# Turning x, y and exp(q) in 32x32 blocks on VectorE, and three iterations for each batch, in a two-layer linear attention

## The chip, the cores and the metric

The kernel runs on one core of one Trainium2 chip. The metric is the device time of one execution in microseconds (us). It is written with one instruction stream for each engine and semaphores between them: TensorE (PE), VectorE (DVE), ScalarE (ACT), GpSimd (POOL) and SyncE (SP), whose only work here is to issue DMAs.

## The reference

Two layers of the same kind run on x, 8 batches of 512 rows and 512 columns (f32), with a condition of 8 x 1024 that gives a scale and a shift for each batch. Layer 0 has 16 heads of 32 columns, layer 1 has 8 of 64. Cut to one layer:

```python
xn = layernorm(x) * norm_scale + norm_bias
q, k, v = xn @ Wq + bq, xn @ Wk + bk, xn @ Wv + bv
k = where(mask, -inf, k)                  # layer 1: k + (1 - mask) * -1e6
v = where(mask, 0, v)                     # layer 1: v * mask
q = softmax(q per head, axis=columns of the head)
k = softmax(k per head, axis=sequence)
attn = einsum('bhse,bhsd->bhed', k, v)
y = einsum('bhtd,bhed->bhte', q, attn)
scale, shift = split(silu(emb) @ film_emb_W + film_emb_b, 2)
h = layernorm(y) * (1 + scale) + shift
return x + silu(h) @ film_out_W + film_out_b
```

## The kernel before

**Tiles.** A batch of x is four tiles of 128 rows (t) by 512 columns; turned, it is four chunks of 128 columns (c) by 512 rows. TensorE contracts over the partition axis, so each operand of a projection must be turned: xT for K, V and Q, the turned q (qT) for the attention, and the turned y for the output projection O. Each f32 operand of a projection is split into a high part (rounded to TensorE's fast 32-bit format) and a low part (the rest), and a product is three passes, high by high, low by high, high by low (L434): 12 products of 512 columns make one tile, 48 a projection.

**Order.** A Python loop, `run_iterations` (L267), writes the order of each engine by hand; the batches 1 to 6 of each layer are a hardware loop (`Fori`) on every engine. There are 16 iterations i, 8 a layer. Iteration i has K, V and Q of batch i, its key-value sums (L643: k_exp by v, 64 or 128 small products into psum_k), the attention built from them by VectorE (L1027 to L1048), the transposes of q on TensorE (`turn_q`, L667), four attends (`attend`, L679: qT by the attention, with a column that sums exp(q)), and between them the four O tiles of batch i-1. The transposes of y (`turn_y`, L507) stand in K and V of the next iteration.

**Turning.** q and y are turned by TensorE with the identity matrix, 128 x 128 each, 16 a batch, into the PSUM tile psum_t; ScalarE copies q from there (L1248) and makes the silu gate from y there (L1187). x is turned by TensorE (L494) in layer 1 and for batches 0 and 1 of layer 0 (ten batches of sixteen in all); for the others the host gives x already turned as well, and VectorE normalises it with rows of mean and 1/std that went through a small tensor in HBM (L752, L754).

**The other engines in an iteration.** VectorE normalises y (L911); takes the greatest k of each tile (L963); makes the key's shift from it, a chain of small steps (L883 to L904, here called the chain) between two block transposes (L875, L904); splits the gate's low parts (L917); subtracts the shift from k (L985); takes the statistics of the next x; biases each q tile out of psum_w (L996) and takes its maxima (L999); builds the attention; adds the output tiles to the residual (L924); and scales each tile of y with the reciprocal of its sum (L1072, L1074). ScalarE masks v out of psum_w (L1218), takes exp of k and q (L1242), scales xT, and makes high parts. GpSimd subtracts q's maxima (L1357), adds the output's bias to the residual (L1323), makes the low parts of x (L1289) and 1/std. psum_w has two halves, used in turn by V, Q and O: a product waits until the tile before last has been taken from its half.

## Time and profile before

| what | value |
|---|---|
| time, median of 3 runs | 865.17 us (863.83 to 866.48) |
| the profiled execution | 866.68 us |
| its span, 16137 instructions | 864.6 us |
| DMA queues | 24700 packets, 78.31 MB |
| granted clock of TensorE, mean | 0.996 |

The span is the profiled time from the first instruction to the last; 2.1 us lie around it. The durations below come from this one execution. Busy time on TensorE is counted by modelled ends of pipelined matmuls: two rows that overlap are read by the distance of their starts. The granted clock is a share of 2.4 GHz: 1.00 is 2.4 GHz and 0.50 is 1.2 GHz.

### The profile page before, as it was taken

What the parts mean: (1) busy time and instruction counts of PE and PEld (TensorE: products, weight loads), DVE (VectorE), ACT (ScalarE), POOL (GpSimd) and SP (SyncE); (2) the same over time, 40 slices, a digit from 0 to 9 for tenths busy, and PEclk for the clock granted to TensorE, in tenths of its full rate; (3) what the DMA queues carried; (4) which work ended last, traced back from release to release, by engine and by line L of the source; (5) the groups of instructions that cost most, each with busy time, mean ns of one, the idle gap of its engine ahead of it and who ended that gap; (6) DMA issues with size and microseconds to landing.
All of it is one profiled execution on the core that took longest, in us unless ns stands there. A gap on an engine that the chain in (4) does not pass through costs nothing.

```text
span 864.6 us, 16137 instructions
## 1 busy us (share of the span) xinstructions
PE 851.0 (98%) x5915; PEld 744.5 (86%) x5915; DVE 619.2 (72%) x1324; ACT 397.6 (46%) x607; POOL 283.6 (33%) x323
## 2 busy tenths in 40 slices
PE   7999999999999999999999999999999999999998
PEld 6678888888888888888888888898888988888887
DVE  6768787877778787777886775667657675575864
ACT  5145445534544553454753634544344433444433
POOL 2032432405243240524313343231433304343520
PEclk8999999999999999999999999999999999999999
DMA  8772222132312213240220403003030120301202
GB/s 270 278 263 99 75 114 81 51 119 73 146 73 111 84 49 121 73 194 14 101 101 1 158 2 133 13 6 139 0 146 0 49 97 0 146 0 58 88 2 97
DMA packets 24700, 78.31 MB, mean 91 GB/s; under 512 B 5464, under 2 KB 5464, under 8 KB 18784
## 3 DMA queue, kind: packets, MB, share of 16 engines
q1 hardware_dynamic: 24672, 77.93, 24.1%
q8 instruction: 18, 0.29, 0.1%
q14 instruction: 10, 0.08, 0.0%
HBM read 61.12 MB, written 16.80 MB: 90 GB/s over the span
## 4 chain that ended last, share of the span: by engine, by line
PE 96%; DVE 2%; DMA 1%; issue 0%; ACT 0%; POOL 0%; SPq 0%; DVEq 0%
PE psum_w L434 58%; PE psum_k L434 20%; PE psum_k L679 6%; PE psum_t L507 3%; PE psum_t L667 3%; PE psum_k L643 3%; PE psum_t L494 2%; DVE y L1074 1%; DMA x_in<-in_x 1%; PE psum_t L459 0%; PE psum_k L459 0%; DVE q_rsum L1072 0%; DVE y_stats L1081 0%; DVE w_low_q L761 0%; PE psum_w L667 0%
## 5 line engine op out<-in xcount | busy, mean ns | idle before, releaser
L1289 POOL TENSOR_TENSOR xT_low<-xT,xT_high 128x512 fp32r<-128x512 f32 x60 | 78.2, 1303 | 168.2 <-ACT xT_high L1148 166.8
L1187 ACT ACTIVATE gate<-psum_t,film_shift,film_scale 128x512 f32<-128x512 f32 x60 | 46.5, 775 | 132.2 <-PE psum_t L507 104.8
L434 PE MATMUL psum_k<-w_high_k,xT_high 128*128 128x512 f32 x256 | 102.0, 399 | 4.5 <-DVE y L1074 2.4
L996 DVE TENSOR_TENSOR q<-psum_w,bias_q 128x512 f32<-128x512 f32 x64 | 44.3, 692 | 80.4 <-PE psum_w L434 80.4
L1273 POOL TENSOR_SCALAR x_var<-x_moments 128x4 f32<-128x4 f32 x15 | 3.4, 228 | 293.1 <-DVE x_moments L733 293.1
L434 PE MATMUL psum_w<-w_high_v,xT_high 128*128 128x512 f32 x256 | 98.7, 386 | 0.0
L434 PE MATMUL psum_k<-w_low_k,xT_high 128*128 128x512 f32 x256 | 98.4, 384 | 0.0
L434 PE MATMUL psum_k<-w_high_k,xT_low 128*128 128x512 f32 x256 | 98.2, 383 | 0.0
L434 PE MATMUL psum_w<-w_high_q,xT_high 128*128 128x512 f32 x256 | 97.5, 381 | 0.0
L434 PE MATMUL psum_w<-w_low_v,xT_high 128*128 128x512 f32 x256 | 97.1, 379 | 0.0
L434 PE MATMUL psum_w<-w_high_v,xT_low 128*128 128x512 f32 x256 | 97.1, 379 | 0.0
L434 PE MATMUL psum_w<-w_low_q,xT_high 128*128 128x512 f32 x256 | 97.1, 379 | 0.0
L434 PE MATMUL psum_w<-w_high_q,xT_low 128*128 128x512 f32 x256 | 97.1, 379 | 0.0
L434 PE MATMUL psum_w<-w_high_o,gT_high 128*128 128x512 f32 x240 | 95.0, 396 | 0.0
L434 PE MATMUL psum_w<-w_low_o,gT_high 128*128 128x512 f32 x240 | 91.0, 379 | 0.0
L434 PE MATMUL psum_w<-w_high_o,gT_low 128*128 128x512 f32 x240 | 91.0, 379 | 0.0
L1242 ACT ACTIVATE q<-q 128x512 f32<-128x512 f32 x64 | 40.4, 631 | 107.2 <-POOL q L1357 107.2
L1218 ACT ACTIVATE v<-psum_w,v_mask 128x512 f32<-128x512 f32 x64 | 44.3, 692 | 91.6 <-PE psum_w L434 91.6
L1357 POOL TENSOR_TENSOR q<-q,q_max 128x512 f32<-128x512 f32 x64 | 67.6, 1075 | 40.4 <-DVE q_max L999 40.4
L1323 POOL TENSOR_TENSOR x_res<-x_res,bias_o 128x512 f32<-128x512 f32 x60 | 75.7, 1293 | 5.7 <-DMA x_res<-x_between_layers 5.7
L1248 ACT COPY qT<-psum_t 128x512 f32<-128x512 f32 x60 | 32.3, 590 | 83.1 <-PE psum_t L667 83.1
L963 DVE SCALAR_TENSOR_TENSOR k_max<-psum_k,k_mask,k_max 128x512 f32<-128x512 f32 x48 | 36.0, 751 | 46.6 <-PE psum_k L434 43.0
(159 smaller groups left out, 1850.1 us busy)
## 6 DMA issues: line engine op xcount, KB each, us to landing
x_in<-x_between_layers SPq DMA_DIRECT2D x9, 1024.0 KB, 4.8
x_res<-in_x SPq DMA_DIRECT2D x8, 1024.0 KB, 6.8
x_between_layers<-x_res SPq DMA_DIRECT2D x8, 1024.0 KB, 3.8
x_in<-in_x SPq DMA_DIRECT2D x7, 1024.0 KB, 4.8
x_res<-x_between_layers SPq DMA_DIRECT2D x7, 1024.0 KB, 6.7
out_x<-x_res SPq DMA_DIRECT2D x7, 1024.0 KB, 3.8
x_in<-in_x_turned SPq DMA_DIRECT2D x6, 1024.0 KB, 5.1
raw_weights<-in_L_cond_film_emb_W SPq DMA_DIRECT2D x4, 1024.0 KB, 7.1
```

What stands on the lines that cost most here:

```text
L434: mm = pe.matmul(bank, lhs[:, c, rows_of_tile], alternating(rhs[w][:, c, :]), start=(c == 0 and n == 0), stop=(c == CHUNKS - 1 and n == 2))
L507: mm = pe.transpose(psum_t[:, c % 2, t, :], y[:, t, c * P:(c + 1) * P], ident[:, :])
L679: mm = pe.matmul(y_psum_of(t)[:, g, 0:BCOLS], qT[:, t, g, :], att_of[layer][:, g, :], start=True, stop=True)
L963: dve.scalar_tensor_tensor(out=k_max[:, :], in0=psum_k[:, t, :], scalar=mask, in1=k_max[:, :], op0=ALU.add, op1=ALU.max).then_inc(k_max_do ...
L996: dve.tensor_tensor(q[:, t, :], psum_w[:, t % 2, :], bias_q[:, :], ALU.add)\
L1187: act.activation(gate[:, c % 2, :], psum_t[:, c % 2, :, :].rearrange("p t s -> p (t s)"), ACT.Silu, scale=film_scale[:, cond, c:c + 1].rea ...
L1218: act.activation(v_of(layer)[:, t, :, 0:width], psum_w[:, t % 2, :].rearrange("p (h n) -> p h n", n=width), ACT.Copy, scale=v_mask[:, bass ...
L1242: act.activation(q[:, t, :], q[:, t, :], ACT.Exp).then_inc(q_exp_ready, 1)
L1248: act.copy(qT[:, t, :, :].rearrange("p c s -> p (c s)"), q_bank(i, t)).then_inc(qT_ready, 1)
L1289: pool.tensor_tensor(xT_low[:, c, :], xT[:, c % 2, :], xT_high[:, c, :], ALU.subtract)\
L1323: pool.tensor_tensor(x_biased, x_biased, bias_o[:, :], ALU.add)\
L1357: pool.tensor_tensor(rows_q, rows_q, q_max[:, t, 0:HEADS[layer]].unsqueeze(2) .to_broadcast([P, HEADS[layer], width]), ALU.subtract).then_ ...
```

## The change

**Three iterations for a batch.** Iteration i now has the projections of batch i in the order K, Q, V; the four attends of batch i-1, after the tiles K2, K3, Q0 and Q1 (a letter and a digit are a projection and its tile t); the key-value sums of batch i; and the output projection of batch i-2. The attention of batch i is built while O of batch i-2 runs. Iterations 0, 1, 2, 6, 7 and 8, 9, 10, 14, 15 are written out, and 3 to 5 and 11 to 13 are loops. The last batch's attends stand between its neighbours' O tiles at the end.

**Turning.** x, y and exp(q) are turned in 32 x 32 blocks within the partitions by VectorE (L784, L793, L801: four instructions of 128 x 512 each a batch), into free parts of raw and k_exp. Sixteen DMAs (`deal`) then put the blocks of one tensor to their partitions, so that xT, yT or qT stands as it did. A deal is issued by SyncE, 16 transfers of 32 partitions x 4 chunks x 128 values (64 KB) each; there are three in an iteration. Before the block transposes ScalarE normalises x and y in their rows (L1294, L1300), with a scale and an offset that GpSimd makes. The last batch's q and y are still turned by TensorE, as are x of batches 0 and 1. The turned x of the host and the rows through HBM are gone.

**What goes with it.** GpSimd takes over the gate's low parts and those of layer 1's weights from VectorE. The gate is made in place in yT. The attends write psum_t, which holds one tile of theirs, where before they had two places in psum_k. Layer 1's weights go through one slot.

```diff
+            def deal(to, blocks, dealt):
+                of_quadrant = blocks.rearrange("p (c d) t j -> p c d (t j)", c=CHUNKS)
+                for frm in range(P // QUAD):
+                    for d in range(P // QUAD):
+                        sp.dma_start(to[d * QUAD:(d + 1) * QUAD, :, frm * P:(frm + 1) * P],
+                                     of_quadrant[frm * QUAD:(frm + 1) * QUAD, :, d, :]).then_inc(dealt[frm], 16)
...
+            def projections(layer, i, att_layer):
...
+                for t in range(TILES):
+                    if t == 0:
+                        pe.wait_ge(att_ready, i)
...
+                        project(i, t, K, psum_k[:, t, :])
+                    if t >= 2:
+                        attend(i - 1, t - 2, att_layer)
...
+                for t in range(TILES):
...
+                    project(i, t, Q, psum_w[:, t % 2, :])
+                    if t < 2:
+                        attend(i - 1, t + 2, att_layer)
...
+                for t in range(TILES):
+                    if t < 2:
+                        pe.wait_ge(q_biased, TILES * i + t + 3)
+                    else:
+                        pe.wait_ge(v_ready, TILES * i + t - 1)
+                    project(i, t, V, psum_w[:, t % 2, :])
...
+            def turn_y_blocks(j, t):
+                if t == 0:
+                    dve.wait_ge(y_normed, TILES * (j + 1))
...
+                dve.transpose(xy_blocks[:, :, t, :], y[:, t, :].rearrange("p (b j) -> p b j", j=QUAD))\
+                   .then_inc(y_blocked, 1)
+            def turn_q_blocks(i, t):
+                if t == 0:
+                    dve.wait_ge(q_exp_ready, TILES * (i + 1))
+                    dve.wait_ge(att_done, i + 1)
+                dve.transpose(q_blocks[:, :, t, :], q[:, t, :].rearrange("p (b j) -> p b j", j=QUAD))\
+                   .then_inc(q_blocked, 1)
-            def normalise_y(j):
-                dve.wait_ge(y_scale_done, 2 * (j + 1))
-                dve.wait_ge(y_moments_done, TILES * (j + 1))
-                for t in range(TILES):
-                    dve.tensor_scalar(y[:, t, :], y[:, t, :], y_moments[:, t, 0:1], y_rstd[:, t:t + 1],
-                                      ALU.subtract, ALU.mult).then_inc(yn_ready, 1)
...
+                take_y(j, att_layer, 3)
+                take_q(i, layer, 1)
+                stats_of_y(j, 3)
+                for t in range(TILES):
+                    moments_of_y(j, t)
+                take_q(i, layer, 2)
+                k_shift_of(i, layer)
+                take_q(i, layer, 3)
+                for t in range(TILES):
+                    turn_y_blocks(j, t)
+                shift_k(i)
+                if normalises_x(i):
+                    x_stats_of(i + 2)
+                if not fixed(i, LAST):
+                    for t in range(TILES):
+                        turn_q_blocks(i, t)
+                if gives_out(i) and not fixed(i, LAST):
+                    add_residual(i - 2, 0)
+                sum_attention(i, layer)
...
+            def low_of_gate(j):
+                high, low = gated_of(j)
+                for c in range(CHUNKS):
+                    pool.wait_ge(g_high_ready, CHUNKS * j + c + 1)
+                    pool.tensor_tensor(low[:, c, :], yT[:, c, :], high[:, c, :], ALU.subtract).then_inc(g_low_ready, 1)
```

**How the instructions move.** On TensorE, in the loop over the batches of layer 0, the second and the third O tile stood so before, with eight transposes of q between them:

```order
L434 MATMUL psum_w<-w_high_o,gT_high 128x512
L434 MATMUL psum_w<-w_low_o,gT_high 128x512
L434 MATMUL psum_w<-w_high_o,gT_low 128x512
L667 MATMUL psum_t<-ident,q 128x128 x8
L434 MATMUL psum_w<-w_high_o,gT_high 128x512
L434 MATMUL psum_w<-w_low_o,gT_high 128x512
```

Now nothing stands between the O tiles, and between K2 and K3 (and three more pairs) there is an attend of the batch before (here in iteration 1, whose x stands in the gate's tiles):

```order
L489 MATMUL psum_k<-w_low_k,gT_high 128x512
L489 MATMUL psum_k<-w_high_k,gT_low 128x512
L581 MATMUL psum_t<-att,qT 128x132 x4
L489 MATMUL psum_k<-w_high_k,gT_high 128x512
L489 MATMUL psum_k<-w_low_k,gT_high 128x512
```

So the attends went from behind the sums of their own batch to the K and Q tiles of the next, and the transposes of q are gone.

Before, the products ahead of the key-value sums were those of the last Q tile, so that v had been masked a whole projection earlier:

```order
L434 MATMUL psum_w<-w_high_q,xT_high 128x512
L434 MATMUL psum_w<-w_low_q,xT_high 128x512
L434 MATMUL psum_w<-w_high_q,xT_low 128x512
L637 REGISTER_ALU
L643 MATMUL psum_k<-v,k_exp 32x34 x64
```

Now they are those of V3:

```order
L489 MATMUL psum_w<-w_high_v,xT_high 128x512
L489 MATMUL psum_w<-w_low_v,xT_high 128x512
L489 MATMUL psum_w<-w_high_v,xT_low 128x512
L720 MATMUL psum_k<-v,k_exp 32x34 x64
L489 MATMUL psum_w<-w_high_o,gT_high 128x512
```

V has moved behind Q: the mask of v tile 3 on ScalarE now stands between the last product and the sums.

On VectorE, between the last k tile's maxima and the subtraction of the key's shift, the chain stood before without any work on q, since Q came after V:

```order
L917 TENSOR_TENSOR gT_low<-gate,gT_high 128x512
L883 TENSOR_REDUCE k_top<-k_turned 128x16
L885 COPY k_top<-k_top 64x16
L886 COPY k_top<-k_top 64x16
L888 TENSOR_TENSOR k_top<-k_top 128x16
L892 COPY k_top<-k_top 32x16 x4
```

Now it stands between the bias adds of the third and the fourth q tile:

```order
L974 TENSOR_TENSOR q<-psum_w,bias_q 128x512
L976 TENSOR_REDUCE q_max<-q 128x16
L941 TENSOR_REDUCE k_top<-k_turned 128x16
L943 COPY k_top<-k_top 64x16
L944 COPY k_top<-k_top 64x16
L946 TENSOR_TENSOR k_top<-k_top 128x16
L950 COPY k_top<-k_top 32x16 x4
L953 TENSOR_TENSOR k_top<-k_top 128x16
L957 TENSOR_TENSOR k_top<-k_top,bias_k 128x16
L959 TENSOR_TENSOR k_top<-bias_k,k_top 128x16
L962 STREAM_TRANSPOSE k_shift_rows<-k_top 128x512
L974 TENSOR_TENSOR q<-psum_w,bias_q 128x512
```

The fourth bias add frees the half of psum_w that V1 needs.

## Rows read from the trace of the kernel before

**Rows 1.** The page, part 1, busy time of each engine.
```profile
PE 851.0 (98%) x5915; PEld 744.5 (86%) x5915; DVE 619.2 (72%) x1324; ACT 397.6 (46%) x607; POOL 283.6 (33%) x323
```

**Rows 2.** Lines of TensorE: busy us, mean ns, idle before.
```profile
L667 PE MATMUL psum_t<-ident,q 128*128 128x128 f32 x240 | 31.2, 273 | 0.3 <-ACT qT L1248 0.3
L507 PE MATMUL psum_t<-ident,y 128*128 128x128 f32 x240 | 31.2, 273 | 0.0
L494 PE MATMUL psum_t<-ident,x_in 128*128 128x128 f32 x144 | 20.2, 273 | 0.0
```

**Rows 3.** Timeline of TensorE: start us, us, form, idle before.
```profile
519.18 1.04 PE L667 MATMUL psum_t<-ident,q 128*128 128x128 f32 x8
519.97 0.46 PE L434 MATMUL psum_w<-w_high_o,gT_high 128*128 128x512 f32 x1
520.27 0.38 PE L434 MATMUL psum_w<-w_low_o,gT_high 128*128 128x512 f32 x1
```

**Rows 4.** Timeline of VectorE, batches 3 and 4.
```profile
206.56 0.16 DVE L1027 COPY att_sums<-psum_k 128x8 f32<-128x8 f32 x1
...
209.88 0.69 DVE L924 TENSOR_TENSOR x_res<-x_res,psum_w 128x512 f32<-128x512 f32 x1
...
257.06 0.15 DVE L1027 COPY att_sums<-psum_k 128x8 f32<-128x8 f32 x1
```

**Rows 5.** Timeline of VectorE, the key's shift in two batches of layer 1.
```profile
545.77 0.68 DVE L883 TENSOR_REDUCE k_top<-k_turned 128x16 f32<-128x512 f32 x1
...
547.10 0.76 DVE L892 COPY k_top<-k_top 32x16 f32<-32x16 f32 x4
...
548.52 0.71 DVE L904 STREAM_TRANSPOSE k_shift_rows<-k_top 128x512 f32<-128x512 f32 x1
549.15 0.65 DVE L917 TENSOR_TENSOR gT_low<-gate,gT_high 128x512 fp32r<-128x512 f32 x1
...
598.58 0.68 DVE L883 TENSOR_REDUCE k_top<-k_turned 128x16 f32<-128x512 f32 x1
```

**Rows 6.** Timeline of VectorE, two tiles of q.
```profile
557.03 0.69 DVE L996 TENSOR_TENSOR q<-psum_w,bias_q 128x512 f32<-128x512 f32 x1 [1.52 <-PE psum_w L434]
...
559.62 0.69 DVE L996 TENSOR_TENSOR q<-psum_w,bias_q 128x512 f32<-128x512 f32 x1 [1.18 <-PE psum_w L434]
```

**Rows 7.** Timeline of TensorE, sums and attend in layer 1's first batch.
```profile
511.88 2.09 PE L643 MATMUL psum_k<-v,k_exp 128*64 128x66 f32 x64
...
523.52 1.18 PE L679 MATMUL psum_k<-att,qT 128*128 128x132 f32 x9
```

**Rows 8.** Timeline of TensorE, from the first sums to batch 1.
```profile
61.05 1.30 PE L643 MATMUL psum_k<-v,k_exp 128*32 128x34 f32 x128
62.28 1.09 PE L494 MATMUL psum_t<-ident,x_in 128*128 128x128 f32 x8
...
71.05 0.48 PE L434 MATMUL psum_k<-w_high_k,xT_high 128*128 128x512 f32 x1 [0.93 <-DVE y L1074]
```

**Rows 9.** Lines of VectorE, the reciprocal of an attend.
```profile
L1072 DVE RECIPROCAL q_rsum<-psum_k 128x16 f32<-128x16 f32 (+1 forms) x64 | 14.7, 230 | 20.9 <-PE psum_k L679 20.8
```

**Rows 10.** Timeline of GpSimd and VectorE, last batch.
```profile
811.65 4.97 POOL L1323 TENSOR_TENSOR x_in<-x_in,bias_o 128x512 f32<-128x512 f32 x4
...
814.22 2.82 DVE L892 COPY k_top<-k_top 32x16 f32<-32x16 f32 x4
```

**Rows 11.** Timeline of ScalarE, the mask of a tile of v.
```profile
549.35 0.69 ACT L1218 ACTIVATE v<-psum_w,v_mask 128x512 f32<-128x512 f32 x1 [1.16 <-PE psum_w L434]
```

**Rows 12.** Timeline of the sync engine's queue.
```profile
9.64 2.28 SPq L335 DMA_DIRECT2D bias_v<-in_L_cond_bv  x4
```

**Rows 13.** The page, part 3: queue, packets, MB, share of 16 engines.
```profile
q1 hardware_dynamic: 24672, 77.93, 24.1%
```

**Rows 14.** Windows: us, each engine's busy (x), PEclk, DMA share, GB/s.
```profile
8.00:13.00 5.00, 2.22 (x16) 1.68 (x16) 3.65 (x7) 2.95 (x5) 3.38 (x10) 0.98 0.91 244
13.00:19.00 6.00, 5.55 (x13) 4.50 (x14) 4.18 (x13) 5.90 (x11) 0.00 (x0) 0.50 1.07 288
```

More of the change, by code:

```diff
@@ L48 @@
 Q, K, V, O = range(4)
[L49 removed]
+SPLIT_ORDER = ((K, V, Q, O), (K, Q, V, O))
 FILM_PARTS = 4
@@ L439, in project, with product @@
-            def project(tiles, m, done, before=None):
-                split_products(tiles, xT_high, xT_low, m, done, before)
+            def product(bank, high, low, m, t, c):
+                for n, (lhs, rhs) in enumerate(((high, w_high), (high, w_low), (low, w_high))):
+                    mm = pe.matmul(bank, lhs[:, c, of_tile(t)], alternating(rhs[m][:, c, :]),
+                                   start=(c == 0 and n == 0), stop=(c == CHUNKS - 1 and n == 2))
+                return mm
+            def project(i, t, m, bank):
+                high, low = x_split_of(i)
+                for c in range(CHUNKS):
+                    mm = product(bank, high, low, m, t, c)
+                mm.then_inc({K: k_psum, V: v_psum, Q: q_psum}[m], 1)
@@ L449, in film_part @@
                 layer, part, half = n // FILM_PARTS, n % FILM_PARTS, n // 2
-                slot, loaded, count = raw_slot(("film", layer, part))
+                slot, loaded, count = raw_slot("film", layer, part)
                 if half >= 2:
@@ new lines, in out_projection, with turn_last_q @@
+            def out_projection(j, t, bank_free, count):
+                pe.wait_ge(bank_free, count)
+                high, low = gated_of(j)
+                for c in range(CHUNKS):
+                    if t == 0:
+                        pe.wait_ge(g_low_ready, CHUNKS * j + c + 1)
+                    mm = product(psum_w[:, t % 2, :], high, low, O, t, c)
+                mm.then_inc(o_psum, 1)
+            def turn_last_q(t):
+                pe.wait_ge(q_exp_ready, TILES * LAST + t + 1)
+                if t >= 2:
+                    pe.wait_ge(qT_ready, t - 1)
+                else:
+                    pe.wait_ge(y_ready, TILES * LAST)
+                for c in range(CHUNKS):
+                    mm = pe.transpose(psum_t[:, t % 2, c, :], q[:, t, c * P:(c + 1) * P], ident[:, :])
+                mm.then_inc(qT_psum, 1)
@@ L670, in attend @@
-                def attend(t):
-                    pe.wait_ge(qT_ready, TILES * i + t + 1)
-                    if t == 0:
-                        pe.wait_ge(att_ready, i + 1)
-                    if t == 1 and first:
-                        pe.wait_ge(film_added, 4)
-                    if t >= 2:
-                        pe.wait_ge(y_ready, TILES * i + t - 1)
-                    for g in range(CHUNKS):
-                        mm = pe.matmul(y_psum_of(t)[:, g, 0:BCOLS], qT[:, t, g, :], att_of[layer][:, g, :],
-                                       start=True, stop=True)
-                    mm.then_inc(y_psum, 1)
@@ L722, in _ @@
+            turn_last_y(3)
+            for t in range(1, TILES):
+                last_out_projection(t)
         @block.vector
@@ L1120, in _, with high_weights @@
+            add_residual(LAST - 1, 0)
+            split_last_gate(0)
+            add_residual(LAST - 1, 1)
+            split_last_gate(1)
+            add_residual(LAST - 1, 2)
+            split_last_gate(2)
+            add_residual(LAST - 1, 3)
+            add_residual(LAST, 0)
+            split_last_gate(3)
+            for t in range(1, TILES):
+                add_residual(LAST, t)
         @block.scalar
         def _(act):
-            def split_weights(layer, n):
-                m = SPLIT_ORDER[n]
-                slot, loaded, count = raw_slot(("weights", layer, m))
+            def high_weights(layer, n):
+                m = SPLIT_ORDER[layer][n]
+                slot, loaded, count = raw_slot("weights", layer, m)
@@ new lines, in iteration @@
+                if not fixed(i, LAST):
+                    low_of_x(i + 1)
+                if normalises_x(i):
+                    x_factors(i + 2)
+                if fixed(i, LAST_0):
+                    low_weights(1)
+                if fixed(i, FIRST_1 + 1):
+                    low_weights(3)
+                    pool.wait_ge(bias_o_loaded, 32)
+            run_iterations(pool, iteration)
+            low_of_gate(LAST - 1)
+            for t in range(TILES):
+                bias_residual(LAST - 1, t)
+                last_scale(t)
@@ L1372 @@
+            for t in range(TILES):
+                bias_residual(LAST, t)
 NAMES = ({Q: "Wq", K: "Wk", V: "Wv", O: "film_out_W"}, {Q: "Wq", K: "Wk", V: "Wv", O: "W_out"})
```

1193 lines of the change are left out of this document (616 added, 577 removed).

## The prediction, made before the changed kernel ran

> **What bounds the kernel now.** I read the page's busy shares first. TensorE is busy 851.0 of 864.6 us, VectorE 619.2, ScalarE 397.6, GpSimd 283.6 [rows 1]; so only TensorE's own work, or a wait put in front of it, moves the end. The lines of TensorE then say what that work is beside the products: 240 transposes of q, 240 of y, 144 of x [rows 2]. In the timeline a group of eight runs from 519.18 to 519.97, 0.79 us, and the product after it takes 0.30 to the next one where 0.216 is usual (2.59 over 12, below) [rows 3]: 0.88 us for eight. The reader is to see that these sit between products with no idle time, so each one removed shortens the span, if nothing takes its place. One batch takes 50.50 us in layer 0 (206.56 to 257.06, rows of `att_sums`) [rows 4] and 52.81 in layer 1 (545.77 to 598.58) [rows 5].
>
> **TensorE's own work after the change.** A tile of 12 products takes 2.59 us (two q tiles, 557.03 and 559.62) [rows 6]; 16 tiles, 41.4. The key-value sums take 2.0 us in layer 1 (2.09 with the tail of the last) [rows 7] and 1.2 in layer 0 (61.05 to 62.28) [rows 8]. Nine instructions of an attend run 1.18 us with their tail [rows 7]; I take 0.9 for the eight of one attend, four times, 3.6. Five returns from such work to products cost 0.09 each [rows 3], 0.4. So 46.7 us for a batch of layer 0 and 47.5 in layer 1: 3.8 and 5.3 under now. Of the 624 transposes 608 go: all 240 of q and 240 of y on these lines, and 128 of x (one batch is still turned on TensorE); the last batch's q, 16, comes back.
>
> **Wait 1, in front of V tile 1.** It needs psum_w's second half, freed by the bias add of q tile 3, which VectorE reaches late, since the chain of the key shift now stands in front of it. From the start of the fourth attend: its result is there after 1.1 (estimate: 0.9 and 0.2 to the consumer); reciprocal and scaling of y, 0.23 [rows 9] and 0.6; q tile 1, 1.3 (two passes of 0.6 to 0.7); statistics of y, 1.0; q tile 2, 1.3; the chain, 3.4 (545.77 to 549.15) [rows 5]; bias add, 0.7. That is 9.7 us. TensorE meanwhile has the attend and Q2, Q3, V0: 8.8. Uncovered: 1.0 us. The chain also meets GpSimd's subtraction of q tile 2. In the last batch, beside four GpSimd passes of 4.97 us, four of the chain's small copies took 2.82 us [rows 10] where they take 0.76 [rows 5]: such an operation ends when the GpSimd pass ends. One pass lies here, about 1.0 us more. I take 2.0; the ends are 1.0 (they miss each other) and 5.1 (the surplus of 2.06 us seen on four small steps, for all eight of the chain).
>
> **Wait 2, in front of the key-value sums.** Before, Q stood between V and the sums; now V is last, and the sums need v tile 3 masked. V1's mask starts 0.28 after TensorE's boundary and takes 0.69 [rows 11]; with the signal 1.1 us. Bounds 0.9 and 1.5.
>
> So a batch takes 49.8 us in layer 0 (0.7 less than now) and 50.6 in layer 1 (2.2 less): three quarters of what the transposes give goes into the two waits.
>
> **The other engines.** VectorE gains 12 block transposes a batch at a pitch of 0.63 us (548.52 to 549.15, 0.71 each) [rows 5], 7.6 us, and loses the splits of the gate and both normalisations. By pitch I count 36 us in 50, so it is not full, and after the key-value sums its order is turn q (2.5), residual, sums and build (3.3, 206.56 to 209.88) [rows 4], ready some 7 us after the sums; the next K0 comes 10.4 later. GpSimd takes over the gate's low parts (four passes of 1.24 [rows 10]) and ScalarE eight normalisations for four copies; both stay near half busy. What TensorE frees on ScalarE (qT) is no longer waited for.
>
> **The DMAs.** Each of three deals a batch is 16 transfers of 64 KB in rows of 512 B, issued by the sync engine. Nothing here moves such rows between SBUF and SBUF. Bounds by issue: four bias_v transfers of small rows took 2.28 us [rows 12], 0.57 each, so a deal takes 9 us, and 48 transfers 27 of 50; an issue alone at 0.34 gives 5.4. Bounds by packets: 24672 packets took 24.1% of 16 engines' 864.6 us [rows 13], 0.135 us each for 3.2 KB; 128 packets per engine and deal cost 2.8 us if time goes with bytes, 17 if with packets. I take 4 and the issue as the limit, since large packets run near bytes. Slack: q is blocked 2.5 us after the sums, and its first quarter, four transfers, is needed 18 us after them; x has 29 us, y about 18. All hidden. The Trainium skill, DMA: Bandwidth & Descriptors, section Bandwidth, lists 0.95 us for a 64 KB transfer and calls transfers below 64 KB dominated by descriptors, advising 1 MiB; by it 48 of them would be 46 us a batch, and with the three whole ones the queue would be over full. No row here shows a 64 KB transfer of such rows; the sum goes by the bounds above.
>
> **Start.** Now the sums end at 62.28 and K0 of batch 1 starts at 71.05 [rows 8]. After: turn q 2.5, sums and build 3.3, signal: 68.3. Then the second attend waits for VectorE, which first splits the O weights, does film and the statistics of x 2, and then waits for GpSimd's factors and ScalarE's normalisation before the first block turn: about 5.2 us (estimate). Batch 1 has no output: 49.8 less 10.4, and with nothing between its sums and the next K0 it waits 6.0 more. K0 of batch 2: 68.3 + 5.2 + 45.4 = 118.9; now 71.05 + 50.5 = 121.6.
>
> **End.** From K0 of batch 15: 24 tiles (K, Q, V and three outputs) 62.2; eight attends 7.2; the last q and y turned on TensorE 3.5; sums 2.0; returns 1.2; waits 2.7; the last add and store 3.7 (estimate from the same kinds): 82.5.
>
> **Clock.** From 13 to 19 us the granted clock is 0.50 (1.2 GHz) [rows 14], after a stretch in which TensorE was busy half the time. Six us at half rate lose 3. The idle stretches of 5 and 6 us at the start may do the same: I take two falls, 6 us; bounds 0 and 9.
>
> **Sum:** 118.9 + 6 x 49.8 + 7 x 50.6 + 82.5 = 854.4, + 6 = 860.4, against the span of 864.6; with what lies around it 862.5 against this execution's 866.7. That execution is 1.5 above the median of 865.17, so I forecast **861 us**.
>
> **Rivals.**
> *Better overlap.* The chain misses GpSimd's pass and the clock holds: 1.0 x 15 and 6 off, 840. For it: GpSimd runs only one pass near the chain. Against: that pass is released by q tile 2, just before the chain.
> *VectorE's chain meets more passes (the slower side).* The place is wait 1. Every further pass costs 1.0 x 15 = 15 us: 876; with all steps blocked, 3.1 x 15, 908. It decides from 0.3 us a batch, since 4 us are all there is to lose. For it: 2.82 against 0.76, and GpSimd has four more passes a batch than now. Against: its residual passes stand behind q tile 3.
> *The deals bound.* At 0.135 us a packet three deals are 52 us and the three whole transfers some 8: 60 us a batch, 15 x 10 more, about 1000. The page's rule above gives 46 + 18 = 64 us, and some 1060. Against both: whole loads already land at the rate of their bytes.
>
> **How the numbers follow.** The forecast's own case, with waits a little off either way, has 0.66: 847 to 878. Better overlap 0.11, the chain 0.19 (half of it inside the range), the deals 0.04. Range 847 to 878. A measurement of this kernel tells about 0.3%, 2.6 us, from no change. Faster: 0.42 of the first and 0.11: 0.53. Same: 0.14 + 0.04 = 0.18. Slower: 0.10 + 0.15 + 0.04 = 0.29.
>
> **What would show it.** TensorE's lines without q and y transposes up to the last batch; distances between `att_sums` of 49.8 and 50.6; TensorE idle before V1 on the q bias add (2.0) and before the sums on ScalarE's mask (1.1); a granted clock of 0.5 somewhere in 70 to 130 us. Wrong it is if TensorE waits for a dealt tile, if K0 waits for the built attention in steady state, or if the small copies of the chain last over 1 us more than once a batch.

## The result, and the profile after

| | before | after |
|---|---|---|
| time, median | 865.09 us (4 runs) | 852.85 us (850.92 to 853.07, 4 runs) |
| ratio, 95% interval | | 0.9853 (0.9832 to 0.9874) |
| profiled execution: span | 864.6 us | 851.2 us |
| granted clock, mean | 0.996 | 0.990 |

The changed kernel is 12.2 us faster, where I had forecast 4.2 (861 us). The direction was right and 852.85 lies in the range, but the size was off by almost three times. The page of the kernel after, busy time of each engine and then the queue that carries the data [rows 1, 13]:

```profile
PE 788.6 (93%) x5307; PEld 681.6 (80%) x5307; DVE 610.0 (72%) x1277; ACT 443.5 (52%) x660; POOL 387.4 (46%) x444
...
q1 hardware_dynamic: 121632, 114.65, 42.8%
```

TensorE is busy for 62.4 us less, and the span is only 13.4 shorter: 49 us are new idle time. What it waits for (the waits of TensorE: us in total, times, longest):

```profile
PE psum_w L489 <- DVE q L974: 23.8, 15, 1.7
PE psum_k L489 <- DVE att L1042: 11.3, 2, 6.5
PE psum_k L720 <- issue: 7.0, 9, 0.8
PE psum_k L720 <- ACT v L1271: 6.4, 6, 1.1
PE psum_t L581 <- issue: 3.1, 1, 3.1
```

The first row is the prediction's wait 1, in front of V1: 15 times, 1.6 each. The third and fourth are its wait 2, in front of the key-value sums: 13.4 us in 15; in the rows marked "issue" too the sums start 0.1 us after the mask of v tile 3 ends (batch 2: the mask from 157.69 to 158.38, the sums at 158.48). The second row is K0 waiting for the built attention, in batches 1 and 2 alone. Of transposes TensorE has these left (the last q, x of batch 1, the last y), where the lines of rows 2 had 624 [rows 2]:

```profile
L602 PE MATMUL psum_t<-ident,q 128*128 128x128 f32 x16 | 2.4, 273 | 0.0
L555 PE MATMUL psum_t<-ident,y 128*128 128x128 f32 x16 | 2.3, 276 | 0.0
L613 PE MATMUL psum_t<-ident,y 128*128 128x128 f32 x16 | 2.2, 272 | 0.0
```

**The span in four stretches**, from the starts of K0. The forecast's 6 us for the clock stand in the second, where it had looked for the falls:

| stretch | forecast | measured | difference |
|---|---|---|---|
| to K0 of batch 1 | 68.3 | 65.25 | -3.0 |
| to K0 of batch 3 | 50.6 + 49.8 + 6.0 | 105.07 | -1.3 |
| to K0 of batch 15 (12 batches) | 603.2 | 598.64 | -4.6 |
| to the end | 82.5 | 82.24 | -0.3 |
| sum | 860.4 | 851.2 | -9.2 |

**Inside one batch** (batch 12, layer 1). TensorE's timeline, the fourth attend, the product behind wait 1, and the sums behind wait 2:

```profile
636.72 1.06 PE L581 MATMUL psum_t<-att,qT 128*128 128x132 f32 x8
...
647.13 0.48 PE L489 MATMUL psum_w<-w_high_v,xT_high 128*128 128x512 f32 x1 [1.58 <-DVE q L974]
...
656.23 0.98 PE L720 MATMUL psum_k<-v,k_exp 128*64 128x66 f32 x26 [1.07 <-ACT v L1271]
```

From the fourth attend to V1 there are 10.4 us, of which TensorE works 8.8, as forecast. What the 10.4 are made of stands in VectorE's timeline, with the GpSimd pass that meets it last:

```profile
642.21 0.68 DVE L941 TENSOR_REDUCE k_top<-k_turned 128x16 f32<-128x512 f32 x1
642.92 0.20 DVE L943 COPY k_top<-k_top 64x16 f32<-64x16 f32 x1
643.16 0.97 DVE L944 COPY k_top<-k_top 64x16 f32<-64x16 f32 x1
644.16 0.17 DVE L946 TENSOR_TENSOR k_top<-k_top 128x16 f32<-128x16 f32 x1
644.37 0.76 DVE L950 COPY k_top<-k_top 32x16 f32<-32x16 f32 x4
...
645.79 0.71 DVE L962 STREAM_TRANSPOSE k_shift_rows<-k_top 128x512 f32<-128x512 f32 x1
646.42 0.65 DVE L974 TENSOR_TENSOR q<-psum_w,bias_q 128x512 f32<-128x512 f32 x1
643.05 1.05 POOL L1461 TENSOR_TENSOR q<-q,q_max 128x512 f32<-128x512 f32 x1
```

The chain runs from 642.21 to 646.42, 4.2 us. Its second small copy (L944) takes 0.97 us, and it ends at 644.13; GpSimd's subtraction of q tile 2 runs from 643.05 to 644.10. The next copies, once GpSimd is through, take 0.19 each. So it waits for the end of the pass, as the forecast had read from the last batch of the kernel before [rows 10].

**The clock.** In these windows (us, busy, granted clock, DMA share, GB/s) it is at 1.2 GHz, behind the idle stretches of 4.8, 3.1 and 6.5 us of iterations 0 and 1:

```profile
66.00:69.00 3.00, 3.00 (x8) 0.50 0.38 97
83.00:86.00 3.00, 3.00 (x9) 0.50 0.41 107
114.00:123.00 9.00, 5.20 (x12) 0.50 0.37 94
```

**The deals.** The sync engine's timeline in batch 12 shows 16 issues of y's deal in 10.27 us, 0.64 each; the three deals take 31 of 50 us of its time:

```profile
650.31 10.27 SPq L389 DMA_DIRECT2D yT<-raw_weights  x16
```

TensorE never waits for a dealt tile in a batch of the steady part. The queue's packets went from 24672 to 121632, and their time from 24.1% to 42.8% of 16 engines' span. The 704 transfers of the deals (240 for q, 240 for y, 224 for x) are 90112 packets of 512 bytes, which the trace has at 0.031 us each; 128 of them per engine and deal are 3.9 us, where I had bounded that by 2.8 and 17 and taken 4. The Trainium skill, page DMA: Bandwidth & Descriptors, section Bandwidth, has 0.95 us for a transfer of 64 KB, by which I had estimated 46 us a batch if one ran behind another. Here one takes a median of 2.0 us from its issue to landing, several are under way at a time, and 16 of them are out in 10.3. That table is of transfers from HBM to SBUF, and these stay within SBUF, so its figure and its rule to transfer 1 MiB at a time aren't tested here like for like; what the trace shows is that the deals are off the path.

### The profile page after: what moved, and what is told of

Read it like the earlier page. It is cut to its first block, busy times and chain, and to the rows that moved or that the text cites. A ratio compares the mean times of both kernels' runs of the same rounds, so it can differ in the third digit from the quotient of the medians.

```text
span 851.2 us, 15057 instructions
## 1 busy us (share of the span) xinstructions
PE 788.6 (93%) x5307; PEld 681.6 (80%) x5307; DVE 610.0 (72%) x1277; ACT 443.5 (52%) x660; POOL 387.4 (46%) x444
## 3 DMA queue, kind: packets, MB, share of 16 engines
q1 hardware_dynamic: 121632, 114.65, 42.8%
## 4 chain that ended last, share of the span: by engine, by line
PE 74%; DVE 17%; issue 4%; ACT 1%; SPq 1%; POOL 1%; DMA 1%; DVEq 0%; POOLq 0%; ACTq 0%
PE psum_w L489 43%; PE psum_k L489 20%; PE psum_t L581 6%; DVE q L974 3%; PE psum_k L720 3%; DVE k_top L944 2%; DVE y L987 1%; DVE k_shift_rows L962 1%; DVE y_stats L994 1%; DVE k_top L941 1%; DVE k_top L950 1%; SPq L389 1%; DVE q_max L976 1%; DVE y_moments L998 1%; DVE k_exp L801 1%
## 5 line engine op out<-in xcount | busy, mean ns | idle before, releaser
L1413 POOL TENSOR_TENSOR gT_low<-yT,gT_high 128x512 fp32r<-128x512 f32 x56 | 71.8, 1285 | 69.9 <-ACT gT_high L1254 66.7
L489 PE MATMUL psum_k<-w_high_k,xT_high 128*128 128x512 f32 x240 | 93.6, 390 | 8.6 <-DVE att L1042 6.5
L1405 POOL TENSOR_TENSOR xT_low<-xT,xT_high 128x512 fp32r<-128x512 f32 x56 | 71.7, 1281 | 57.1 <-ACT xT_high L1208 53.5
L489 PE MATMUL psum_k<-w_low_k,xT_high 128*128 128x512 f32 x240 | 92.2, 384 | 0.0
L489 PE MATMUL psum_k<-w_high_k,xT_low 128*128 128x512 f32 x240 | 92.0, 383 | 0.0
L489 PEld LDWEIGHTS psum_w<-w_high_v,xT_high 128*128 128x128 f32 x240 | 45.3, 189 | 36.0 <-DVE q L974 27.6
L1004 DVE TENSOR_TENSOR x_res<-x_res,psum_w 128x512 f32<-128x512 f32 x56 | 38.5, 688 | 47.5 <-PE psum_w L489 47.3
L581 PEld LDWEIGHTS psum_t<-att,qT 128*128 128x128 f32 x480 | 63.2, 190 | 6.6 <-issue 3.4
L801 DVE STREAM_TRANSPOSE k_exp<-q 128x512 f32<-128x512 f32 x60 | 37.4, 680 | 42.6 <-PE psum_k L720 42.6
L1300 ACT ACTIVATE raw_weights<-raw_weights,x_offset,x_rstd 128x512 f32<-128x512 f32 x56 | 41.0, 802 | 50.5 <-POOL x_offset L1383 50.5
```

The lines of the kernel that those rows point to most:

```text
L489: mm = pe.matmul(bank, lhs[:, c, of_tile(t)], alternating(rhs[m][:, c, :]), start=(c == 0 and n == 0), stop=(c == CHUNKS - 1 and n == 2))
L581: mm = pe.matmul(y_bank_of(j, t)[:, g, 0:BCOLS], q_columns[:, g, :], att_of[layer][:, g, :], start=True, stop=True)
L801: dve.transpose(q_blocks[:, :, t, :], q[:, t, :].rearrange("p (b j) -> p b j", j=QUAD))\
L1004: dve.tensor_tensor(x_sum, x_sum, psum_w[:, t % 2, :], ALU.add).then_inc(o_added, 1)
L1300: act.activation(x_rows[:, t, :], x_rows[:, t, :], ACT.Identity, scale=x_rstd[:, t:t + 1], bias=x_offset[:, t:t + 1]).then_inc(x_normed, 1)
L1405: pool.tensor_tensor(low[:, c, :].rearrange("p (t a j) -> p t a j", t=TILES, j=QUAD), scaled_x(i, c), high[:, c, :].rearrange("p (t a j) - ...
```

## The experiments

Times are medians. All were compared with the kernel before on the same chip (863.6 to 865.4 us); the changed kernel itself is 852.85.

### The chain behind q tile 3

```diff
                 take_q(i, layer, 2)
-                k_shift_of(i, layer)
                 take_q(i, layer, 3)
+                k_shift_of(i, layer)
```

> The edit moves one call on VectorE: the key's shift (the chain) goes behind the bias add and maxima of q tile 3. Theory A, the wait in front of V1 (1.65 us in layer 0, 1.58 in layer 1, 15 times, 23.8 us with the last) is only that chain in front of the bias add: the wait goes, the chain ends 1.3 us later against the k exponentials, whose last ends 1.3 before the last mask of v, so the wait in front of the sums stays near 1.0; 852.8 less 22 gives 831 us, with 0 to 5 coming back in front of the sums. Rival B, the wait is only moved, since the shifted k come later than v: the idle time before the sums grows by about the 1.6 that goes, and the time stays between 848 and 853.

Measured: **920.06 us**, ratio 1.0644 (1.0621 to 1.0667). The wait before V1 is gone, and both theories were wrong on what comes in its place. VectorE's chain and GpSimd's passes in batch 11:

```profile
636.89 0.68 DVE L941 TENSOR_REDUCE k_top<-k_turned 128x16 f32<-128x512 f32 x1
637.60 0.53 DVE L943 COPY k_top<-k_top 64x16 f32<-64x16 f32 x1
638.16 1.21 DVE L944 COPY k_top<-k_top 64x16 f32<-64x16 f32 x1
639.40 1.20 DVE L946 TENSOR_TENSOR k_top<-k_top 128x16 f32<-128x16 f32 x1
640.64 2.83 DVE L950 COPY k_top<-k_top 32x16 f32<-32x16 f32 x4
...
644.13 0.71 DVE L962 STREAM_TRANSPOSE k_shift_rows<-k_top 128x512 f32<-128x512 f32 x1
637.05 1.04 POOL L1461 TENSOR_TENSOR q<-q,q_max 128x512 f32<-128x512 f32 x1 [0.39 <-DVE q_max L976]
638.05 1.28 POOL L1455 TENSOR_TENSOR x_res<-x_res,bias_o 128x512 f32<-128x512 f32 x1
```

The first copy ends with the subtraction of q tile 3. Behind it four additions of the output's bias stand back to back, and each of the next four small steps ends with one of them: 1.21, 1.20, and two of the four copies that take 2.83 together. What comes after the last pass (643.04) is short again. The chain takes 7.9 us in place of 3.4. Then the sums wait, and the clock falls behind that wait (timeline and window of TensorE):

```profile
651.86 0.38 PE L720 MATMUL psum_k<-v,k_exp 128*64 128x66 f32 x2 [5.98 <-ACT v L1271]
650.00:655.00 5.00, 3.14 (x57) 0.50 0.41 104
```

A batch takes 54.3 to 54.9 us, about 4.7 more than in the changed kernel: 1.6 less before V1, 4.9 more before the sums, and the rest is work at half the clock. This is the mechanism of the prediction's slower rival, and at its full price: it had 908 us for all small steps blocked. But that rival had the wait in front of V1, and here it stands in front of the sums. That the changed kernel is faster rests on where GpSimd's four passes stand.

### No GpSimd pass on the chain

```diff
                     y_factors(i - 1)
+                    pool.wait_ge(k_shift_rows_ready, i + 1)
                 shift_q(i, layer, 2)
```

> The edit holds GpSimd's subtraction of q tile 2 until the key's shift is done; VectorE's order stays. Theory A, a small VectorE copy that meets a GpSimd pass waits for its end: the second copy of the chain falls from 0.97 us to 0.2, the wait before V1 from 1.6 to 0.8, and the time by 15 x 0.8 = 12 us to 841. Rival B, the copy's 0.97 us comes from something else (its own length, ScalarE's or a DMA's traffic): it stays at 0.97 and the time within 2 us of 852.8. Rival C, the later exponential of q tile 2 holds back the masks of v on ScalarE, and TensorE waits before V2 instead: the copy is short, the time is 848 or more.

Measured: **839.87 us**, 0.9715 (0.9698 to 0.9732). Theory A. The lines of VectorE have the copy at 169 ns, where the changed kernel has it at 920; the waits of TensorE have wait 1 at 0.8 each:

```profile
L944 DVE COPY k_top<-k_top 64x16 f32<-64x16 f32 x16 | 14.7, 920 | 0.5
```

```profile
L944 DVE COPY k_top<-k_top 64x16 f32<-64x16 f32 x16 | 2.7, 169 | 0.5
PE psum_w L489 <- DVE q L974: 11.7, 15, 0.8
```

In layer 0 a batch takes 48.85 us in place of 49.65. So the meeting of one pass and one copy cost 0.8 us a batch, 12 to 13 us in the whole, and what is left of wait 1 is the chain itself, with the other work that VectorE has between the attend and V1. The Trainium skill, page SBUF — State Buffer, section Who interferes with whom, says that VectorE contends with GpSimd in a mode that takes two ports, and with two SBUF inputs contends with a GpSimd instruction that reads SBUF; the shared ports are an exclusive lock, and in the two-port mode whoever comes second blocks for the other's whole instruction. The trace of the run before agrees: the copies and L946, the greater of two SBUF operands, end with a pass (1.21 and 1.20 us in place of 0.17), and the reduction ahead of them (L941), with one input, keeps its 0.68 us beside GpSimd's pass. In which mode the copies run no trace shows.

### The chain behind q tile 3, the residual held

```diff
                 if gives_out(i):
+                    pool.wait_ge(k_shift_rows_ready, i + 1)
                     for t in range(TILES):
                         bias_residual(i - 2, t)
```

> As the first run (the chain behind q tile 3), and GpSimd's four additions of the output's bias wait until the key's shift is done. In the first run they stood beside the chain, its eight small steps took 5.9 us in place of 1.9, and TensorE waited 5.8 to 6.0 us before the sums, with the granted clock at 0.5 behind each wait. Theory A, the chain lost that time to the GpSimd passes alone: the chain takes about 4.5 us (one pass, that of q tile 3, still meets it), nothing waits before V1, about 1 to 2 us before the sums, and the time is 829 to 838 us. Rival B, the chain's place is the cause (it is too late behind q tile 3 whatever GpSimd does): the wait before the sums stays above 4 us a batch and the time above 890.

Measured: **839.43 us**, 0.9701 (0.9682 to 0.9721), just above the range of theory A and far from B. VectorE and TensorE in the batch:

```profile
631.86 0.53 DVE L943 COPY k_top<-k_top 64x16 f32<-64x16 f32 x1
632.42 0.17 DVE L944 COPY k_top<-k_top 64x16 f32<-64x16 f32 x1
632.63 0.18 DVE L946 TENSOR_TENSOR k_top<-k_top 128x16 f32<-128x16 f32 x1
632.84 0.76 DVE L950 COPY k_top<-k_top 32x16 f32<-32x16 f32 x4
641.99 0.51 PE L720 MATMUL psum_k<-v,k_exp 128*64 128x66 f32 x10 [1.85 <-ACT v L1271]
```

One pass meets one copy (0.53), the others are short again. The place behind q tile 3 was not what cost 67 us; the passes were. The wait is now before the sums, 1.6 to 1.9 a batch, so the chain's own length shows up there.

### K, V, Q again

One part of the change undone on all engines: V stands before Q, with the attends after K2, K3, V0 and V1. Of TensorE's part:

```diff
-                    project(i, t, Q, psum_w[:, t % 2, :])
+                    project(i, t, V, psum_w[:, t % 2, :])
                     if t < 2:
                         attend(i - 1, t + 2, att_layer)
...
                 for t in range(TILES):
                     if t < 2:
-                        pe.wait_ge(q_biased, TILES * i + t + 3)
+                        pe.wait_ge(v_ready, TILES * i + t + 3)
                     else:
-                        pe.wait_ge(v_ready, TILES * i + t - 1)
-                    project(i, t, V, psum_w[:, t % 2, :])
+                        pe.wait_ge(q_biased, TILES * i + t - 1)
+                    project(i, t, Q, psum_w[:, t % 2, :])
```

VectorE does the chain, then the subtraction of the shift, then the q tiles with y's block transposes between them; GpSimd adds two tiles' bias between q tiles 1 and 2 and two after 3.

> The edit undoes one part of the change, the order of the projections: K, V, Q again, with the attends between K2, K3, V0 and V1, and the work of VectorE, ScalarE and GpSimd put in the order that this asks for. Theory A, both waits of a batch (1.6 before V1, 1.0 before the sums) come from V standing last: both go, TensorE's own work of 46.9 us in layer 0 and 47.6 in layer 1 is left, 14 batches x 2.65 = 37 us less, 816 us. Rival B, q is now late: its last tile is biased 0.3 after the last product, then 1.05 on GpSimd and 0.63 on ScalarE, its block transposes, its deal of 16 transfers at 0.64 us each; either the first attend waits for a dealt quarter, or K0 waits for the built attention or for the low parts of x behind GpSimd's residual passes. At 1 us a batch that gives 830, at 2.6 us a batch no gain, 853.

Measured: **820.82 us**, 0.9495 (0.9477 to 0.9513), 32 less than the changed kernel. Both waits are gone, and a batch takes 47.33 us in either layer. The five microseconds that are missing from theory A stand mainly in three rows: batches 1 and 2 now wait 4.8 and 8.8 us for the built attention, where the changed kernel waits 4.8 and 6.5; at the end the transposes of the last y wait for their normalisation; and in six batches of layer 0 an O tile waits 0.3 to 0.5 us for VectorE's residual addition:

```profile
PE psum_k L489 <- DVE att L1046: 13.5, 2, 8.8
...
PE psum_t L613 <- DVE y L1051: 2.9, 2, 2.3
...
PE psum_w L489 <- DVE x_res L1008: 2.0, 6, 0.5
```

Beyond that the late q costs nothing. So both waits come from V's place, with the order of the other engines' work that goes with it, as the prediction argued.

### q's deal in halves

```diff
+                        for part in range(parts):
+                            cs = slice(part * CHUNKS // parts, (part + 1) * CHUNKS // parts)
+                            sp.dma_start(to[d * QUAD:(d + 1) * QUAD, cs, frm * P:(frm + 1) * P],
+                                         of_quadrant[frm * QUAD:(frm + 1) * QUAD, cs, d, :])\
+                              .then_inc(dealt[frm], 16)
...
-                    deal(qT[:, :, :, :].rearrange("p a c n -> p a (c n)"), q_blocks, q_dealt)
+                    deal(qT[:, :, :, :].rearrange("p a c n -> p a (c n)"), q_blocks, q_dealt, 2)
```

> The edit splits each transfer of q's deal in two of 32 KB, 32 in place of 16, with the same rows and bytes. Theory A, the deals are far from the bound and an issue costs the sync engine 0.64 us whatever its size: the deal of q takes 20.5 us to issue in place of 10.3, the three deals 41 of 50 us, and still nobody waits: 852 to 854 us. Rival B, an issue costs by its rows: the deal keeps 10.3 us, time the same. Rival C, the deals are near the bound: the last quarter of q lands too late for the fourth attend or x's deal is pushed into its use, and each batch takes 1 to 5 us more, 865 or more.

Measured: **860.83 us**, 0.9962 (0.9948 to 0.9976). The sync engine's timeline in batch 11, and at the change of the layers; then TensorE's there:

```profile
618.36 20.88 SPq L391 DMA_DIRECT2D qT<-k_exp  x32
```

```profile
411.71 21.44 SPq L391 DMA_DIRECT2D qT<-k_exp  x32
433.20 0.58 SPq L420 DMA_DIRECT2D x_between_layers<-x_res  x1
433.83 0.43 SPq L370 DMA_DIRECT2D raw_weights<-in_L_cond_Wv  x1
448.75 0.77 PE L492 MATMUL psum_w<-w_high_v,xT_high 128*128 128x512 f32 x1 [6.28 <-issue]
```

An issue of 32 KB costs 0.65 us, as much as one of 64 KB (20.88 us for 32). The period of the steady batches is unchanged, 49.4 to 50.2, so theory A holds there; 7.4 of the 8 us are in one place that none of the three had, batch 8, which takes 57.4 us in place of 50.0. The load of layer 1's V weights is queued behind q's deal of batch 7 (433.83, in the changed kernel 424.23), ScalarE waits for it until 443.03, GpSimd makes the last low part of these weights until 448.65, and V0, the first tile that needs them, starts at 448.75, 6.3 us late; the rest is work at half the clock behind that wait (0.50 from 447 to 453). The three deals take 41 of 50 us of the sync engine here, and nobody waits for them in a steady batch; what is issued once behind them is late all the same.

### The clock: TensorE kept busy in the three waits

```diff
+            def keep_busy(n):
+                for _ in range(n):
+                    pe.matmul(psum_w[:, 0, 0:P], ident[:, :], ident[:, :], start=True, stop=True)
...
+                    if fixed(j, 0) and t == 1:
+                        keep_busy(26)
...
                     turn_film(3)
+                    pe.wait_ge(q_biased, 3)
+                    keep_busy(42)
+                if fixed(i, 1):
+                    keep_busy(58)
```

> The changed kernel, with products of the identity matrix by itself (42, 26 and 58 of 128 columns, into a free half of psum_w, read by nobody) in the three long waits of iterations 0 and 1, where TensorE stood idle for 4.8, 3.1 and 6.5 us. Theory A, the granted clock falls to 0.5 behind these waits because TensorE is idle in them: the stretches at 0.5 from 66 to 69, 83 to 86 and 114 to 123 us go, 1.7, 1.7 and 2.9 us less, 846.5 us. Rival B, they fall for another reason: the clock keeps its dents and the time stays at 852.8, or rises by 1 to 3 where the added products outlast a wait.

Measured: **861.51 us**, 0.9964 (0.9950 to 0.9977), slower than the changed kernel: a product took 0.227 us, twice what I had counted, and they outlasted the waits. So theory A holds for the clock and not for the time. The clock stayed at 1.00 from 60 to 130 us. The same on K, V, Q, with the same mistake in it:

> The order K, V, Q with the same added products in the three waits (there the last is 8.8 us). Theory A: the same 5 to 6 us less than with K, V, Q alone (820.8), 815 us. Rival B: no gain, 820 to 822. If only the first two stretches are held, since 58 products fill about 6 of the 8.8 us of the last, 817 to 818.

Measured: **828.93 us**, 0.958 (0.9567 to 0.9593), 8 more than without. Then the fitted numbers on the changed kernel, 19, 12 and 27:

> The changed kernel with the added products again, fewer: one of them took 0.227 us in the run before (84 instructions in 9.54 us), not the 0.11 I had sized them by, so 42, 26 and 58 outlasted the waits by 5 to 7 us each, though the granted clock then stayed at 1.00 from 60 to 130 us. Now 19, 12 and 27, 4.3, 2.7 and 6.1 us for waits of 4.8, 3.1 and 6.5. Theory A, idle TensorE in the waits is what the clock's falls follow: the clock stays at 1.00 and the time is 852.85 less 5 to 6, 847. Rival B, the falls come back with the short idle rests that are left, or their cost is smaller than I count: 850 to 853.

Measured: **853.59 us** (852.83 to 855.56), 0.9867 (0.9850 to 0.9884), no faster than the changed kernel. Its windows and one row of TensorE's timeline:

```profile
66.00:71.00 5.00, 4.83 (x22) 1.00 0.38 96
110.00:117.00 7.00, 6.56 (x93) 1.00 0.39 99
117.00:124.00 7.00, 6.95 (x32) 1.00 0.37 94
```

```profile
357.14 0.27 PE L726 MATMUL psum_k<-v,k_exp 128*32 128x34 f32 x2 [2.60 <-issue]
```

From the first sums to K0 of batch 3 it takes 107.94 us, against 112.59 in the changed kernel: 4.65 less, near the 5 to 6 expected, and the clock is at 1.00 throughout, so theory A holds for the falls. It is given back at two places. This execution comes to the first sums 0.9 us later (58.63, against 57.73), since it waits 1.19 us and not 0.43 at the film products. And in batch 6, in the middle of the sums, TensorE stands for 2.60 us with nothing that the profile names as awaited, the clock falls again (0.50 from 357 to 360), and that batch takes 53.75 us in place of 49.44. The trace has one transfer of its queue for instructions inside that stop, 16 KB from 354.88 to 355.81, with the stop from 354.54 to 357.14; in the changed kernel the transfers of that queue next to the same sums begin at 349.05 and 359.22, and nothing stops. That TensorE waited for its own instructions is thus likely, and not shown. All five runs took about the same (852.83 to 855.56), so the stop probably belongs to this program, though one run alone was traced.

### The attention built first in iterations 0 and 1

```diff
-                for t in range(TILES):
-                    turn_q_blocks(0, t)
                 sum_attention(0, 0)
                 build_attention(0, 0)
+                for t in range(TILES):
+                    turn_q_blocks(0, t)
```

and the same in iteration 1, ahead of the statistics of x 3; on top of K, V, Q.

> The order K, V, Q, and in iterations 0 and 1 alone VectorE builds the attention before it turns q in blocks (and in 1 before the statistics of x 3). Theory A, K0 of batches 1 and 2 waits for the built attention behind that other work: K0 of batch 1 comes 2.4 us sooner, K0 of batch 2 another 2.5 to 5, less 0 to 3 that come back where x 3 is then late for its block transposes; 812 to 817 us. Rival B, the deal of q or x 3 is late instead and takes it all back: 820 to 822.

Measured: **817.02 us**, 0.9449 (0.9436 to 0.9462). K0 of batch 1 comes at 62.30 (65.66 without), K0 of batch 2 at 112.76 (117.43), and 0.8 comes back by batch 3: theory A, at the dear end.

### All that helped, together

> The version that the runs so far point to: the order K, V, Q, the attention built first in iterations 0 and 1, and 7, 21 and 15 added products in its three waits of 1.9, 5.4 and 4.0 us. From 817.0, less the clock lost behind these waits (read from the windows: 1.5, 2.9 and 2.4 us): 811 us. If the falls stay, 817; if the added products outlast a wait, 812 to 815.

Measured: **815.43 us** (813.77 to 820.05, 6 runs), 0.9431 (0.9406 to 0.9457), not the 811 expected, but the fastest of all, 37 us under the changed kernel. Against the version without added products the difference, 1.6 us, is within the two intervals. The clock held at 1.00 from 60 to 130 us. From the first sums to K0 of batch 3 it takes 101.36 us, against 104.86 without the added products: 3.5 less, where 6.8 had been counted, with 2.3 us of idle time left in front of the second attend. And 1.7 of the 3.5 are hidden in the profiled execution, since its granted clock from 13 to 19 us was 0.72 where that of the version without was 1.00; it comes to the first sums at 59.35, not 57.65. The next section has that fall.

### The kernel before, once more

> The kernel before, unchanged, profiled a second time, for the stretch from 13 to 19.5 us in which its granted clock was 0.50. In six profiles of its successors, with the same 2.07 us of idle TensorE ahead of it, the clock of that stretch was 1.00 in two, 0.72 in three and 0.50 in one. Theory A, the depth of that fall varies from one execution to the next: a value other than 0.50 comes with a span shorter by up to 3 us. Rival B, it belongs to the kernel before: 0.50 and 864.6 us again, and the 3.3 us by which the changed kernel is ahead when the first sums begin are a gain of the change.

Measured: 864.56 us, span 862.4. The window of its start and the start of batch 1 [rows 8, 14]:

```profile
13.00:19.00 6.00, 5.64 (x26) 1.00 0.94 299
68.85 0.48 PE L434 MATMUL psum_k<-w_high_k,xT_high 128*128 128x512 f32 x1 [0.93 <-DVE y L1074]
```

The clock did not fall, with 2.08 us of idle time ahead of this stretch as before. K0 of batch 1 came at 68.85, not 71.05. Theory A. What the fall costs shows at the film products, in the first and the second profile of the kernel before and in the changed kernel:

```profile
30.92 1.07 PE L459 MATMUL psum_t<-raw_weights,emb_cols 128*32 128x512 f32 x8 [0.43 <-DVE emb_cols L968]
28.71 1.06 PE L459 MATMUL psum_t<-raw_weights,emb_cols 128*32 128x512 f32 x8 [1.37 <-DMA raw_weights<-in_L_cond_film_emb_W]
27.61 1.06 PE L516 MATMUL psum_t<-raw_weights,emb_cols 128*32 128x512 f32 x8 [0.43 <-DVE emb_cols L1063]
```

Without the wait in front of them TensorE comes there 17.04, 13.98 and 13.99 us after its first K0 (13.45, 13.36 and 13.19): the fall costs 3.1 us, and nothing of that is the change. In the run with the chain behind q tile 3, whose clock there was 0.72, it is 15.66, so that fall costs 1.7. The ten executions of the kernel before on this chip lie in three groups at that distance: 863.4 to 863.5 us with a mean granted clock of 1.000, 865.1 to 865.5 with 0.998, 866.5 to 866.7 with 0.996. The first profile (866.68) is like the last of them; the second (864.56) is like the first, with 0.9 us more of waiting for the film weights.

## Why the prediction came out as it did

**Direction and mechanism: right.** TensorE bound the kernel and does so now; the transposes of q and y went, and in steady state nothing but the two forecast waits stands between its products. Its own work of a batch is 50.24 - 2.65 = 47.6 us in layer 1 (forecast 47.5) and 46.9 in layer 0 (46.7). That V's place makes both waits, and that one GpSimd pass lies on the chain, was shown by undoing each.

**Size: wrong, since the forecast gain was a small difference of large terms**, and the three that were off most erred the same way. On the span the misses add up to 9.2 us:

- *Wait 1 and wait 2*: 2.0 and 1.1 us a batch forecast, 1.6 and 0.95 measured. The pass cost 0.8, not 1.0, and the uncovered rest was 0.8, not 1.0. Over the 12 batches of the steady part wait 1 was 4.65 us too dear (19.35 measured) and wait 2 1.8 (11.4), 6.5 together, of which 1.9 went back as own work that I had counted short: 4.6. This is the largest miss.
- *The start*: 3.0 us. The step "Now the sums end at 62.28 and K0 of batch 1 starts at 71.05" took the profiled execution of before as the kernel's own start. It held a fall of the clock from 13 to 19.5 us that cost 3.1, and the second profile shows the same kernel without one. I carried that fall into the forecast, and wrote a 3 us loss down for it in the part on the clock, without asking whether it recurs. In the profile of the changed kernel it is absent, and that is the whole 3.0. The second profile of before is only 2.2 us earlier since it waits 0.9 us longer for the film weights' transfer (1.37, against 0.43), a wait that varies between executions: it is 0.43 in the changed kernel and 1.19 in the run with the fitted products. The last step of the forecast, from 862.5 to 861, took half of the fall off again, by going from this execution to the median.
- *The clock*: "I take two falls, 6 us". There were three, and filling the waits gave back 4.65. So 6 was 1.3 too much, inside its bounds of 0 and 9. That the middle of the bounds was near is in part luck: how many falls come was not derived.
- *The end* was within 0.3.

The steps that failed are thus two terms of the sum: the price of the waits, "I take 2.0" for wait 1 above all, where 1.6 was measured, and the start of batch 1 at 68.3 us, where 65.25 was measured. With the first, "three quarters of what the transposes give goes into the two waits" fell for layer 1: the transposes gave 5.2 and the waits took 2.65, half. In layer 0 it held (2.7 of 3.6). With the waits and the own work of the steady batches as measured (4.6 less), the start at 65.25 and 4.65 us for the clock the sum is 851.5, against the span of 851.2.

**The rivals.** *Better overlap* had 840 us for a chain that misses the pass and a clock that holds. The run that arranged the first measured 839.87, but that the numbers meet is luck: the meeting cost 0.8 a batch and not 1.0, the clock still fell behind the waits of iterations 0 and 1 (0.50 at 66 to 69 and at 114 to 123 us), and the 861 that the rival was counted from was 8 too high. *The chain meets more passes* had 908: moving the chain by one step measured 920, with the wait in front of the sums in place of V1 and the falls of the clock on top. Its chance (0.19) was a fair price for a danger that is real one step away, but the argument against it, that the residual passes stand behind q tile 3, was decisive for the kernel as it is. *The deals bound* (0.04) had 1000: nobody waits for them in steady state. The issue is 0.64 us each, just outside my upper bound of 0.57, and the packets of a deal take 3.9 us where I had taken 4.

**Open.** What the q and y transposes alone would give without the new pipeline was not tried. What stopped TensorE for 2.60 us in the run with the fitted products isn't shown (a transfer of instructions fell into it), and the granted clock of the stretch from 13 to 19.5 us (1.00, 0.72 or 0.50 in the profiles of like starts) is not explained by anything that the traces show ahead of it.

## What to carry to other kernels

A saving on the bounding engine is worth what the new order leaves of it: here 49 of 62 us went into waits, and putting V before Q again gave 32 of them back. Before placing a chain of small VectorE steps, look at what GpSimd runs beside it: each meeting of a copy or a step with two SBUF operands cost the rest of a pass, and five passes in a row turned a 3.4 us chain into 7.9. When a forecast is a difference of large terms, take the baseline from two profiles, so that a fall of the clock in one of them isn't priced as a property of the kernel.

## What was not expected of the hardware

- A transfer of 64 KB or 32 KB, in rows of 512 bytes within SBUF, costs the sync engine 0.64 to 0.65 us to issue in the quoted rows, where whole tensors mostly take 0.34 to 0.6.
- A product of the 128 x 128 identity by itself in f32 took 0.227 us (84 instructions, two for each, in 9.54), about as much as one of 512 columns of the split operands (0.216).
- With the same idle time of 2.07 us ahead, the granted clock from 13 to 19 us was 1.00 in five of thirteen profiles (the kernel before at its second profile, the changed kernel, K, V, Q, the attention first, the fitted products), 0.72 in six and 0.50 in two (the kernel before at its first profile and the changed kernel with too many added products). It costs 0, 1.7 or 3.1 us.
